# Two-layer graph kernel: new beginning, attention end and end of layer 1's loop

## Chip, cores and metric

One core of a Trainium2 chip runs the whole kernel. The time is device microseconds of one execution; three runs of the kernel before gave 675.48 to 677.48, with a median of 676.37.

## What is computed

```python
# layer 0
deg = clip(adj.sum(axis=1), 1);  dis = deg ** -0.5
diffusion = (dis[:, None] * adj * dis[None, :]) @ x - x
norms = maximum(norm(x), 1e-8)
attn = softmax(beta * (x @ x.T / (norms[:, None] * norms[None, :])) * adj, axis=1)
x = layernorm(x + diffusion + sigmoid(alpha) * (attn @ x - x))
# layer 1
XW = x @ W;  s_col = XW @ a[0, :128];  s_row = XW @ a[0, 128:]
den = exp(leaky_relu(s_row[:, None] + s_col[None, :], 0.01))
num = adj @ den;  att = where(num != 0, den / num, 0)
out = layernorm(x + adj @ (att @ XW))
```

x is 2708 x 128, adj 2708 x 2708 of zeros and ones. The host hands over adj transposed and both padded to 2816 = 22 x 128 rows.

## The kernel before

There are T = 22 tiles of 128 rows (the last has 20) and NC = 6 column pieces of 452 (the last 448). Every engine has its own instruction stream, written out by hand and tied by semaphores; `Waiting.wait_ge` leaves out a wait that an earlier one covers.

**Beginning.** SP loads x (L333), W, a, the row constants, beta and alpha in one queue. POOL issues the 22 loads of adjT, which turn float32 into 8-bit floats in AT (L358): four at once, eighteen after its power. ScalarE squares x (L543), VectorE sums (L786), POOL takes the root by a power (L385), VectorE inverts it and multiplies x by it, four tiles at a time (L800). TensorE transposes the result into two PSUM banks in turn (L1433); ScalarE copies it as float16 (L546), VectorE subtracts this copy for the low half (L797). Then ScalarE makes xh, the bfloat16 copy of x (L547), VectorE and POOL its remainder xl (L806, L389), VectorE the scale of x (`scale_of`, L776 to L782), the sigmoid of alpha and a flag whether beta is large (L810 to L820). Every engine branches on that flag into its `attention` body.

**Layer 0's loop** runs over NU = 132 units, 22 rows jt of six pieces c, through a ring of six buffers. A unit is: three float16 matmuls for the logits on TensorE (L1441), a product with the adjacency on VectorE (L908), Exp on ScalarE (L560), an addition into the row sums ES on POOL (L401; L399 copies in row 0), for four of six pieces the low half of the result on VectorE (L913), and the product with x on TensorE, three bfloat16 matmuls (L1496) or, for the pieces of FULL = (2, 5), one float32 matmul (L1486). In piece 0 of each row 22 one-column matmuls count degrees (L1477), which VectorE adds up (L897). In the last row come the roots of the degrees (`roots`, L855 to L863; Ln and Exp at L563, L565), the scaled x (`scaled`, L869) and its two float16 halves xp (L568, L876).

**Behind the loop** ScalarE and VectorE bring six banks to AOT (L572, L931), POOL splits ES into bfloat16 halves (L416, L418), and TensorE transposes W (L1582), multiplies the first tile's diffusion (`spread(0)`, L1515), transposes AOT (L1596) and sums ES over partitions (`row_sums`, L1571). VectorE needs these sums for all rows of the attention (L987, L991). ScalarE scales x (L591) and later makes `emptied` (L599). The layer norm, the ranking of keys and the windows of layer 1 follow.

**Layer 1's loop** has 66 steps; in each ScalarE takes Ln (L731) and Exp (L709), VectorE the scores (L1322) and the low half (L1329), TensorE sums (L1708) and products (L1768). Behind the branch VectorE multiplies the result (L1378, L1383) into YT, reduces all of it by minimum and maximum (L1387, L1388), combines them (L1390) and calls `scale_of(1, ...)`. TensorE transposes YT meanwhile (L1804), ScalarE and VectorE scale it into two float16 halves (L764, L1395), and 484 matmuls (L1809) give the output, with the layer norm behind each tile.

## Time and profile before

| | |
|---|---|
| median of three runs | 676.37 us |
| the profiled execution | 675.03 us |
| its span, first to last instruction | 673.3 us |
| busy PE, DVE, ACT, POOL | 569.4, 544.2, 352.8, 435.7 us |
| mean granted TensorE clock | 0.944 |

Busy time is given by engine: PE is TensorE, DVE VectorE, ACT ScalarE, POOL GpSimd, SP the queue of plain DMAs. The span leaves out what lies before the first and behind the last instruction, 1.7 us here. A row of the trace names the line of the kernel before.

### The profile page before, as it was taken

What the parts mean: (1) busy time and instruction counts of PE and PEld (TensorE: products, weight loads), DVE (VectorE), ACT (ScalarE), POOL (GpSimd) and SP (SyncE); (2) the same over time, 40 slices, a digit from 0 to 9 for tenths busy, and PEclk for the clock granted to TensorE, in tenths of its full rate; (3) what the DMA queues carried; (4) which work ended last, traced back from release to release, by engine and by line L of the source; (5) the groups of instructions that cost most, each with busy time, mean ns of one, the idle gap of its engine ahead of it and who ended that gap; (6) DMA issues with size and microseconds to landing.
All of it is one profiled execution on the core that took longest, in us unless ns stands there. A gap on an engine that the chain in (4) does not pass through costs nothing.

```text
span 673.3 us, 11277 instructions
## 1 busy us (share of the span) xinstructions
PE 569.4 (85%) x4123; PEld 348.4 (52%) x4123; DVE 544.2 (81%) x965; ACT 352.8 (52%) x568; POOL 435.7 (65%) x448
## 2 busy tenths in 40 slices
PE   0489999999998679999718988898989999949993
PEld 0245555455453368888617644344445444427883
DVE  1679999999999973678888766899898999985442
ACT  2334544444443542579986226787777788811000
POOL 5849999999998933556305043687786788203663
PEclk9999999999999589999757989999999999988997
DMA  9999891000000000000000041323242333000000
GB/s 148 101 108 108 108 380 51 0 1 1 1 1 1 5 1 17 18 24 17 18 1 21 5 125 46 77 82 103 63 110 72 91 95 98 21 5 13 29 28 18
DMA packets 17797, 37.21 MB, mean 55 GB/s; under 512 B 2570, under 2 KB 8222, under 8 KB 17726
## 3 DMA queue, kind: packets, MB, share of 16 engines
q0 software_dynamic: 7392, 24.32, 20.2%
q1 hardware_dynamic: 10334, 11.98, 5.4%
q8 instruction: 39, 0.64, 0.4%
q14 instruction: 32, 0.26, 0.1%
HBM read 48.72 MB, written 10.45 MB: 88 GB/s over the span
## 4 chain that ended last, share of the span: by engine, by line
PE 35%; POOL 25%; DVE 22%; issue 7%; ACT 7%; DMA 2%; DVEq 0%; POOLq 0%; ACTq 0%; SPq 0%
POOL R L401 23%; PE PSALL L1809 8%; PE PSALL L1708 5%; PE PSALL L1515 5%; DVE ring L1329 4%; DVE ring L1322 4%; ACT AW L629 4%; PE PSALL L1637 3%; PE PSALL L1768 3%; PE PSALL L1441 2%; DVE FR L1329 2%; DVE FR L1322 1%; PE PSALL L1716 1%; PE PSALL L1538 1%; DMA X<-in_x 1%
## 5 line engine op out<-in xcount | busy, mean ns | idle before, releaser
L401 POOL TENSOR_TENSOR R<-R,ring 128x452 f32<-128x452 f32 (+1 forms) x126 | 174.9, 1424 | 5.5 <-ACT ring L560 5.5
L560 ACT ACTIVATE ring<-ring,sm 128x452 f32<-128x452 f32 (+1 forms) x132 | 85.0, 669 | 106.0 <-DVE ring L908 105.9
L913 DVE TENSOR_TENSOR AW<-ring 128x452 bf16<-128x452 f32 (+1 forms) x88 | 105.2, 1196 | 0.0
L1441 PE MATMUL PSALL<-XN 128*128 128x452 f16 (+2 forms) x396 | 99.0, 361 | 5.5 <-issue 4.2
L1708 PE MATMUL PSALL<-AW,R 128*128 128x452 fp8e4 (+1 forms) x348 | 78.4, 357 | 16.6 <-DVE R L1261 10.3
L908 DVE TENSOR_TENSOR ring<-PSALL,AT 128x452 f32<-128x452 f32 (+1 forms) x132 | 78.6, 616 | 3.3 <-PE PSALL L1441 2.9
L463 POOL DMA_INDIRECT AW<-ATd,FR x44 | 55.3, 1258 | 31.7 <-DVE FR L1212 17.1
L1768 PE MATMUL PSALL<-ring,XW 128*128 128x452 bf16 (+1 forms) x300 | 67.7, 360 | 0.9 <-DVE ring L1329 0.9
L1441 PEld LDWEIGHTS PSALL<-XN 128*128 128x128 f16 (+1 forms) x396 | 37.6, 98 | 58.1 <-issue 25.4
L1329 DVE TENSOR_TENSOR ring<-ring 128x904 bf16<-128x904 f32 (+1 forms) x50 | 62.6, 1252 | 0.0
L1515 PE MATMUL PSALL<-R,AT 128*128 128x256 f16 x484 | 61.6, 287 | 0.0
L1708 PEld LDWEIGHTS PSALL<-AW,R 128*128 128x128 bf16 x348 | 32.4, 98 | 56.1 <-DVE R L1261 17.2
L1809 PE MATMUL PSALL<-R,AT 128*128 128x256 f16 x484 | 55.1, 279 | 2.0 <-DVE R L1395 2.0
L1496 PE MATMUL PSALL<-ring,AO 128*128 128x452 bf16 (+1 forms) x176 | 50.3, 367 | 4.4 <-DVE AW L913 3.2
L1515 PEld LDWEIGHTS PSALL<-R,AT 128*128 128x128 fp8e4 x484 | 48.8, 103 | 7.8
L1809 PEld LDWEIGHTS PSALL<-R,AT 128*128 128x128 fp8e4 x484 | 48.3, 100 | 8.6 <-DVE R L1395 2.1
L709 ACT ACTIVATE ring<-ring,st 128x904 f32<-128x904 f32 (+1 forms) x50 | 52.3, 1046 | 0.3 <-DVE ring L1322 0.3
L731 ACT ACTIVATE R<-PSALL,sm 128x452 f32<-128x452 f32 x66 | 38.5, 635 | 24.0 <-PE PSALL L1716 20.7
L731 ACT ACTIVATE TL<-PSALL,sm 128x452 f32<-128x452 f32 x66 | 38.5, 635 | 19.7 <-PE PSALL L1716 17.5
L1768 PEld LDWEIGHTS PSALL<-ring,XW 128*128 128x128 bf16 x300 | 28.6, 96 | 31.6 <-DVE ring L1329 2.0
L1322 DVE SCALAR_TENSOR_TENSOR ring<-R,st,TL 128x904 f32<-128x904 f32 (+1 forms) x33 | 38.4, 1162 | 7.2 <-ACT TL L731 6.7
L629 ACT ACTIVATE AW<-R 128x128 bf16<-128x128 bf16 (+21 forms) x30 | 42.7, 1422 | 2.2 <-DVE R L1008 0.4
(262 smaller groups left out, 1035.3 us busy)
## 6 DMA issues: line engine op xcount, KB each, us to landing
AT<-in_adjT POOLq DMA_DIRECT2D x22, 338.5 KB, 32.6
ATd<-AT SPq DMA_DIRECT2D x2, 3723.5 KB, 16.6
XWd<-ring SPq DMA_DIRECT2D x11, 128.0 KB, 1.8
out<-ring SPq DMA_DIRECT2D x21, 64.0 KB, 1.5
AW<-ATd,FR POOLq DMA_INDIRECT x44
X<-XWd,idx POOLq DMA_INDIRECT x22, 2.6
Wt<-in_W SPq DMA_DIRECT2D x1, 64.0 KB, 11.0
X<-in_x SPq DMA_DIRECT2D x1, 0.5 KB, 7.8
```

The source lines that it names most:

```text
L401: i = G.tensor_tensor(ES_, ES_, z, ALU.add)
L560: S.activation(z, z, ACT.Exp, scale=bcol[0:rows, :]).then_inc(s_exp, 1)
L731: S.activation(tL[v % 2][:, q * RW:(q + 1) * RW], PSALL[:, 6 + q, 0:RW], ACT.Ln, bias=tiny).then_inc(s_ln, 1)
L908: V.tensor_tensor(z, PSALL[0:rows, b, 0:w], A_, ALU.mult).then_inc(s_z, 1)
L913: V.tensor_tensor(Fl[q % 6][0:rows, 0:w], ring[0:rows, q % 6, 0:w], upper(q, rows, w), ALU.subtract).then_inc(s_low, 1)
L1322: V.scalar_tensor_tensor(z_of(v), rb[:, c0:c0 + w], negc[:, v // 3:v // 3 + 1], tL[v % 2][:, 0:w], ALU.max, ALU.subtract).then_inc(s_sub, 1)
L1329: V.tensor_tensor(lower, z_of(v), high, ALU.subtract).then_inc(s_alo, 1)
L1441: m = TE.matmul(PSALL[0:rows, b, 0:w], lh[:, jt * P:jt * P + rows], rh[:, c0:c0 + w], start=(k == 0), stop=(k == 2))
L1515: ins = TE.matmul(PSALL[:, it % 4, 0:2 * D], AT[:, jt, it * P:(it + 1) * P], xp[:, jt, :, :].rearrange("p c d -> p (c d)"), start=(jt == 0 ...
L1708: TE.matmul(PSALL[:, b, 0:w], den_h[:, s + 1 + q, :, part], AW[:, jt % 3, q, c0:c0 + w], start=(q == 0 and part == 1), stop=False)
L1768: m = TE.matmul(PSALL[:, c, 0:CH[c][1]], XW2[:, jt % 4, part, :], att[:, part_of], start=(jt == 0 and k == 0), stop=(jt == T - 1 and k == 2))
L1809: return TE.matmul(PSALL[:, out_bank[it], 0:2 * D], AT[:, jt, it * P:(it + 1) * P], xpY[:, jt, :, :].rearrange("p c d -> p (c d)"), start= ...
```

## The change

- x is loaded in two halves, then beta and alpha, then the rest. POOL issues all adjacency loads once both halves of x are there.
- Squares and sums come in four pieces. POOL's power becomes Ln and Exp on ScalarE with a correcting step on VectorE. ScalarE makes two of the six groups of normalised rows; the transposes use four banks; scale, flag and sigmoid are put between the other steps. POOL makes all of xl, the last 18 tiles behind its first six units.
- Logits wait for the low halves that they read, not for all. Degree groups of rows 16 to 21 move to piece 3 of rows 10 to 15.
- Roots move to unit 102. ScalarE makes the scaled x tile by tile in units 105 to 115 and its high halves after that; VectorE makes the low halves in units 121, 123, 127 and 129.
- The last row leaves POOL: its Exp results are split into LH and LL (all six pieces), which TensorE sums with ESh and ESl, 88 matmuls instead of 44. POOL splits ES after 126 units, into other buffers.
- ScalarE takes five banks to AOT, VectorE one. `spread(0)` waits for its bank alone; the transposes of AOT wait for all; the transpose of W comes behind them.
- VectorE's steps from the products of layer 1 to the halves of the result stand inside the branch bodies. ScalarE takes absolute values per pair of pieces, VectorE one maximum each.
- The second semaphore chain s_dve2 becomes s_dve throughout.

```diff
-        ESh, ESl = XN[:, 0:NP // 2].bitcast(BF16)[:, 0:N], XN[:, NP // 2:NP].bitcast(BF16)[:, 0:N]
+        ESh, ESl = EM[:, :].bitcast(BF16)[:, 0:N], AWflat[:, 6 * RW:6 * RW + N]
+        LH, LL = (FR[0:LAST, q * N // 2:(q + 1) * N // 2].bitcast(BF16) for q in range(2))
...
+        QT = ((0, 6), (6, 5), (11, 6), (17, 5))
+        NE = NU - NC
+        DEGREES = {(t, 0): t for t in range(16)}
+        DEGREES.update({(10 + t, 3): 16 + t for t in range(T - 16)})
+        DEG_NO = {u: n for n, u in enumerate(u for u in UNITS if u in DEGREES)}
+        LOWS = [20 * NC + 1, 20 * NC + 3, NE + 1, NE + 3]
+        XD = 17 * NC + 3
...
-            q(X3, x.rearrange("(t p) d -> p t d", p=P)).then_inc(s_x, 16)
+            for h in range(2):
+                q(X3[:, h * 11:(h + 1) * 11, :],
+                  x[h * 11 * P:(h + 1) * 11 * P, :].rearrange("(t p) d -> p t d", p=P)).then_inc(s_x[h], 16)
+            q(braw, beta.broadcast_to([P, 1])).then_inc(s_beta, 16)
+            q(araw, alpha.broadcast_to([P, 1])).then_inc(s_beta, 16)
...
-            for t in range(4):
-                load_AT(t)
...
-            gp.wait_ge(s_sq, 2)
-            G.tensor_tensor(nrm, sq, half.broadcast_to([P, T]), ALU.pow).then_inc(s_norm, 1)
-            for t in range(4, T):
+            for h in range(2):
+                gp.wait_ge(s_x[h], 16)
+            for t in range(T):
                 load_AT(t)
             gp.wait_ge(s_xh, 1)
-            G.tensor_tensor(xl[:, 4:T, :], X3[:, 4:T, :], xh[:, 4:T, :], ALU.subtract).then_inc(s_xlrest, 1)
+            G.tensor_tensor(xl[:, 0:4, :], X3[:, 0:4, :], xh[:, 0:4, :], ALU.subtract).then_inc(s_xlfirst, 1)
+
+            def low_rest(k):
+
+                t0 = 4 + 3 * k
+                G.tensor_tensor(xl[:, t0:t0 + 3, :], X3[:, t0:t0 + 3, :], xh[:, t0:t0 + 3, :], ALU.subtract).then_inc(s_xlrest, 1)
 
             def attention(shifted):
                 if shifted:
...
-                for u, (jt, c) in enumerate(UNITS):
+                for u, (jt, c) in enumerate(UNITS[:NE]):
...
+                    if jt == 0:
+                        low_rest(c)
...
-            gp.wait_ge(s_esum, NU)
-            gp.wait_ge(s_logit, NU)
+            gp.wait_ge(s_esum, NE)
             G.tensor_copy(ESh, ES[:, 0:N]).then_inc(s_es, 1)
             gp.wait_ge(s_es, 1)
             G.tensor_tensor(ESl, ES[:, 0:N], ESh, ALU.subtract).then_inc(s_es, 1)
-            gp.wait_ge(s_aotA, 3)
-            gp.wait_ge(s_aotD, 3)
             G.memset(AOT[:, N:NP], 0.0).then_inc(s_pad, 1)
             for it in range(T):
...
+            av.wait_ge(s_beta, 32)
+            S.activation(eal, araw, ACT.Exp, scale=-1.0).then_inc(s_ealpha, 1)
+            for h, (t0, nt) in enumerate(QT):
+                av.wait_ge(s_x[h // 2], 16)
+                S.activation(xx[:, t0:t0 + nt, :], X3[:, t0:t0 + nt, :], ACT.Square).then_inc(s_early, 1)
+            av.wait_ge(s_sq, 5)
+            S.activation(deg, sq, ACT.Ln).then_inc(s_norm, 1)
+            av.wait_ge(s_norm, 1)
+            S.activation(rn, deg, ACT.Exp, scale=-0.5).then_inc(s_norm, 1)
+
+            def normal_rows(g):
+
+                t0, nb = GRP[g]
+                av.wait_ge(s_sq, 6)
+                for t in range(t0, t0 + nb):
+                    i = S.activation(AO3[:, t, :], X3[:, t, :], ACT.Copy, scale=rn[:, t:t + 1])
+                i.then_inc(s_early, 1)
+
+            def rows_high(g):
+
+                t0, nb = GRP[g]
                 av.wait_ge(s_xnT, g + 1)
-                S.activation(xnh[:, t0 * P:(t0 + nb) * P], PSALL[:, g % 2, 0:nb * P], ACT.Copy).then_inc(s_xnh, 1)
+                S.activation(xnh[:, t0 * P:(t0 + nb) * P], PSALL[:, g % 4, 0:nb * P], ACT.Copy).then_inc(s_xnh, 1)
+
+            normal_rows(1)
...
+            normal_rows(1)
+            rows_high(0)
+            normal_rows(4)
+            for g in range(1, 6):
+                rows_high(g)
             S.activation(xh, X3, ACT.Copy).then_inc(s_xh, 1)
...
+            def scaled_rows(t0, nt):
+
+                av.wait_ge(s_dis, 4)
+                for t in range(t0, t0 + nt):
+                    S.activation(xd3[:, t, :], X3[:, t, :], ACT.Copy, scale=dup[:, t:t + 1]).then_inc(s_xd, 1)
+
+            def scaled_high(k):
+
+                t0, nt = SL[k]
+                av.wait_ge(s_xd, t0 + nt)
+                S.activation(xp[:, t0:t0 + nt, 0, :], xd3[:, t0:t0 + nt, :], ACT.Copy).then_inc(s_xphi, 1)
 
...
+                    if not shifted and 0 <= u - XD < T // 2:
+                        scaled_rows(2 * (u - XD), 2)
+                    if not shifted and 0 <= u - XD - T // 2 < len(SL):
+                        scaled_high(u - XD - T // 2)
+                    if jt == T - 1:
+                        av.wait_ge(s_exp, u + 1)
+                        S.activation(LH[:, CH[c][0]:CH[c][0] + w], upper(u, rows, w), ACT.Copy).then_inc(s_lh, 1)
...
+                for c in range(NC - 1):
                     c0, w = CH[c]
+                    av.wait_ge(s_gather, NE + c + 1)
                     S.activation(AOT[:, c0:c0 + w], PSALL[:, c, 0:w], ACT.Copy).then_inc(s_aotA, 1)
...
+            av.wait_ge(s_rsum, 1)
...
+            for p in range(3):
+                c0, w = wide_of(p)
+                av.wait_ge(s_YTd, 2 * p + 2)
+                S.activation(YA[:, c0:c0 + w], YT[:, c0:c0 + w], ACT.Abs).then_inc(s_yhi, 1)
...
+            V.tensor_scalar(sq, sq, COS_EPS * COS_EPS, None, ALU.max).then_inc(s_sq, 1)
+            dv.wait_ge(s_beta, 32)
+            V.tensor_scalar(bcol, braw, 1.0 / (XS * XS), None, ALU.mult).then_inc(s_bcol, 1)
+            k = own.step(V.tensor_tensor(beta2, braw[0:1, :], braw[0:1, :], ALU.mult))
             dv.wait_ge(s_dve, k)
-            k = own.step(V.reciprocal(rn, nrm))
+            k = own.step(V.tensor_scalar(beta2, beta2, BETA_PLAIN ** 2, None, ALU.is_gt))
             dv.wait_ge(s_dve, k)
-
-            def split_low(g):
+            V.tensor_copy(flag[:, :], beta2).then_inc(s_flag, 1)
+            dv.wait_ge(s_norm, 2)
+            k = own.step(V.tensor_tensor(dis, rn, rn, ALU.mult))
+            dv.wait_ge(s_dve, k)
+            k = own.step(V.tensor_tensor(dis, dis, sq, ALU.mult))
+            dv.wait_ge(s_dve, k)
+            k = own.step(V.tensor_scalar(dis, dis, -0.5, 1.5, ALU.mult, ALU.add))
+            dv.wait_ge(s_dve, k)
+            V.scalar_tensor_tensor(rn, dis, XS, rn, ALU.mult, ALU.mult).then_inc(s_sq, 1)
+            dv.wait_ge(s_sq, 6)
+
...
+            normal_rows(0)
+            k = own.step(V.scalar_tensor_tensor(nrm, sq, 1.0 / (XS * XS), rn, ALU.mult, ALU.mult))
+            normal_rows(2)
+            dv.wait_ge(s_dve, k)
             V.tensor_reduce(pm, nrm, AX.X, ALU.max).then_inc(s_pm, 1)
-            scale_of(0, (PSALL[0:1, 5, 0:P], PSALL[:, 5, 0:1]), XS, up_x, down_x)
+            rows_low(0)
+            normal_rows(3)
+            dv.wait_ge(s_scale, 1)
+            k = own.step(V.tensor_reduce(top, PSALL[0:1, 5, 0:P], AX.X, ALU.max))
+            rows_low(1)
+            dv.wait_ge(s_dve, k)
+            V.tensor_scalar(top, top, 1e-30, None, ALU.max).then_inc(s_top, 1)
+            normal_rows(5)
+            rows_low(2)
+            rows_low(3)
+            dv.wait_ge(s_scale, 2)
+            k = own.step(V.tensor_scalar(down_x, PSALL[:, 5, 0:1], XS * 2.0 ** -14, None, ALU.mult))
+            rows_low(4)
+            dv.wait_ge(s_dve, k)
+            V.reciprocal(up_x, down_x).then_inc(s_up, 1)
+            rows_low(5)
             dv.wait_ge(s_ealpha, 1)
             k = own.step(V.tensor_scalar(eal, eal, 1.0, None, ALU.add))
             dv.wait_ge(s_dve, k)
...
+                    if u == 17 * NC:
+                        roots()
+                    if not shifted and u in LOWS:
+                        scaled_low(LOWS.index(u))
...
+            def products_out():
+
+                dv.wait_ge(s_sub, NV)
+                dv.wait_ge(s_erb, 1)
+                for p in range(3):
+                    c0, w = wide_of(p)
+                    dv.wait_ge(s_y, NV - 3 + p + 1)
+                    if w == 2 * RW:
+                        V.tensor_tensor(YT[:, c0:c0 + w].rearrange("p (q w) -> p q w", q=2), PSALL[:, 2 * p:2 * p + 2, 0:RW],
+                                        erb[:, c0:c0 + w].rearrange("p (q w) -> p q w", q=2), ALU.mult).then_inc(s_YTd, 2)
+                    else:
+                        for c in (2 * p, 2 * p + 1):
+                            c0, w = CH[c]
+                            V.tensor_tensor(YT[:, c0:c0 + w], PSALL[:, c, 0:w], erb[:, c0:c0 + w], ALU.mult).then_inc(s_YTd, 1)
+                    if p == 0:
+                        V.memset(orow, 1.0)
+                for p in range(3):
+                    c0, w = wide_of(p)
+                    dv.wait_ge(s_yhi, p + 1)
+                    k = own.step(V.tensor_reduce(ln[:, p:p + 1], YA[:, c0:c0 + w], AX.X, ALU.max))
+                dv.wait_ge(own.sem, k)
+                V.tensor_reduce(pm, ln[:, 0:3], AX.X, ALU.max).then_inc(s_pm, 1)
+
+            def transposed_out():
+
+                scale_of(1, (PSALL[0:1, 6, 0:P], PSALL[:, 6, 0:1]), 1.0, up_y, down_y)
+                dv.wait_ge(s_up, 2)
+                for g, (t0, nb) in enumerate(GRP):
+                    dv.wait_ge(s_yhi, 3 + g + 1)
+                    V.scalar_tensor_tensor(xpY[:, t0:t0 + nb, 1, :], PSALL[:, g, 0:nb * P].rearrange("p (b d) -> p b d", b=nb), up_y,
+                                           xpY[:, t0:t0 + nb, 0, :], ALU.mult, ALU.subtract).then_inc(s_ylo, 1)
 
             table(2)
             where["any"] = eng.value_load(win[0:1, 2 * T:2 * T + 1], min_val=0, max_val=1)
...
-            own.step(V.tensor_reduce(up_y, YT, AX.X, ALU.min))
-            k = own.step(V.tensor_reduce(down_y, YT, AX.X, ALU.max))
-            dv.wait_ge(s_dve2, k)
-            V.scalar_tensor_tensor(pm, up_y, -1.0, down_y, ALU.mult, ALU.max).then_inc(s_pm, 1)
...
+            turn(0)
+            turn(1)
+            pe.wait_ge(s_pm, 1)
+            TE.transpose(PSALL[0:1, 5, 0:P], pm, ident[:, :]).then_inc(s_scale, 1)
+            turn(2)
+            turn(3)
+            pe.wait_ge(s_top, 1)
+            TE.matmul(PSALL[:, 5, 0:1], orow, top, start=True, stop=True).then_inc(s_scale, 1)
+            turn(4)
+            turn(5)
 
...
-                pe.wait_ge(s_xnl, 6)
+                pe.wait_ge(s_xnl, max((c0 + w - 1) // (4 * P), jt // 4) + 1)
...
+                if it < 4:
+                    pe.wait_ge(s_aotA, it + 1)
...
+                pe.wait_ge(s_aotA, NC - 1)
+                TE.transpose(PSALL[:, 4, 0:P], Wt[:, :], ident[:, :]).then_inc(s_wT, 1)
                 pe.wait_ge(s_es, 2)
+                pe.wait_ge(s_lh, NC)
+                pe.wait_ge(s_low, low_no(NU - 1))
+                pe.wait_ge(s_aotD, 1)
                 for t in range(T):
                     rows = rows_of(t)
-                    for k, part in enumerate((ESh, ESl)):
-                        m = TE.matmul(PSALL[0:rows, 5, t:t + 1], part[:, t * P:t * P + rows], ones[:, :],
-                                      start=(k == 0), stop=(k == 1))
+                    for k, (part, high) in enumerate(((ESh, P), (ESl, P), (LH, LAST), (LL, LAST))):
+                        m = TE.matmul(PSALL[0:rows, 5, t:t + 1], part[0:high, t * P:t * P + rows], ones[0:high, :],
+                                      start=(k == 0), stop=(k == 3))
                 m.then_inc(s_rsum, 1)
```

## Rows read from the trace of the kernel before

**Rows 1.** Page, chain that ended last, shares by line

```profile
POOL R L401 23%; PE PSALL L1809 8%; PE PSALL L1708 5%; PE PSALL L1515 5%; DVE ring L1329 4%; DVE ring L1322 4%; ACT AW L629 4%; PE PSALL L1637 3%; PE PSALL L1768 3%; PE PSALL L1441 2%; DVE FR L1329 2%; DVE FR L1322 1%; PE PSALL L1716 1%; PE PSALL L1538 1%; DMA X<-in_x 1%
```

**Rows 2.** Chain of waits in order, beginning: start us, us, what

```profile
0.86 7.82 DMA X<-in_x
...
13.35 3.91 POOL st L385
...
34.85 1.04 issue
```

**Rows 3.** Timeline, beginning: start, us, engine, line, out<-in, count [idle before]

```profile
26.66 1.02 DVE L797 TENSOR_TENSOR XN<-PSALL,XN 128x512 f16<-128x512 f32 x2 [0.90 <-ACT XN L546]
...
29.44 5.04 POOL L389 TENSOR_TENSOR AO<-X,AO 128x2304 bf16<-128x2304 f32 x1 [2.61 <-ACT AO L547]
...
37.95 0.61 DVE L908 TENSOR_TENSOR ring<-PSALL,AT 128x452 f32<-128x452 f32 x1
```

**Rows 4.** DMA issues (last column us to landing); start of the ATd stores

```profile
sm<-in_alpha SPq DMA_DIRECT2D x1, 0.5 KB, 19.7
...
L339 SPq DMA_DIRECT2D ATd<-AT x2: 389/914/1439, 82.2 to 82.6; - x2
```

**Rows 5.** Timeline inside layer 0's loop, VectorE one row apart; POOL's in an early row

```profile
101.86 0.61 DVE L908 TENSOR_TENSOR ring<-PSALL,AT 128x452 f32<-128x452 f32 x1
...
110.03 0.61 DVE L908 TENSOR_TENSOR ring<-PSALL,AT 128x452 f32<-128x452 f32 x1
...
46.56 1.15 POOL L401 TENSOR_TENSOR R<-R,ring 128x452 f32<-128x452 f32 x1 [1.27 <-ACT ring L560]
```

**Rows 6.** Chain of waits in the loop's first rows, degree groups

```profile
44.44 0.53 PE PSALL L1477 x22
...
52.38 0.54 PE PSALL L1477 x22
```

**Rows 7.** Timeline, the end of layer 0's attention

```profile
195.34 16.87 POOL L401 TENSOR_TENSOR R<-R,ring 128x452 f32<-128x452 f32 x12
...
212.84 1.01 DVE L855 TENSOR_TENSOR st<-st 128x22 f32<-128x22 f32 x1
...
215.42 0.24 DVE L863 TENSOR_SCALAR st<-st,sm 128x22 f32<-128x22 f32 x1
...
222.94 3.61 DVE L876 TENSOR_TENSOR R<-R 128x768 f16<-128x768 f32 x3
...
223.57 1.70 PE L1486 MATMUL PSALL<-ring,X 20*128 20x448 f32 x2
...
225.80 3.06 POOL L416 CAST XN<-R 128x2708 bf16<-128x2708 f32 x1
...
228.49 4.75 PE L1515 MATMUL PSALL<-R,AT 128*128 128x256 f16 x22
...
234.64 1.33 PE L1571 MATMUL PSALL<-ones,XN 128*128 128x1 bf16 x44 [0.52 <-POOL XN L418]
...
236.65 6.54 ACT L599 ACTIVATE EM<-ident,FR 128x128 bf16<-128x128 f32 x22
```

**Rows 8.** Windows: busy us of PE, PEld, DVE, ACT, POOL, granted clock, DMA, GB/s

```profile
180.00:200.00 20.00, 19.78 (x149) 9.98 (x147) 20.00 (x31) 9.54 (x15) 20.00 (x16) 1.00 0.00 1
...
226.00:236.00 10.00, 7.22 (x76) 5.61 (x76) 8.78 (x8) 4.09 (x7) 8.63 (x3) 0.65 0.02 5
```

**Rows 9.** Page's group L709; timeline at the end of layer 1

```profile
L709 ACT ACTIVATE ring<-ring,st 128x904 f32<-128x904 f32 (+1 forms) x50 | 52.3, 1046 | 0.3 <-DVE ring L1322 0.3
...
591.33 2.58 PE L1768 MATMUL PSALL<-ring,XW 128*128 128x452 bf16 x12 [0.95 <-DVE ring L1329]
...
594.49 2.11 DVE L1378 TENSOR_TENSOR R<-PSALL,R 128x904 f32<-128x904 f32 x2 [2.00 <-PE PSALL L1768]
...
597.72 3.06 DVE L1387 TENSOR_REDUCE sm<-R 128x1 f32<-128x2816 f32 x1
...
603.81 0.16 DVE L1390 SCALAR_TENSOR_TENSOR sm<-sm 128x1 f32<-128x1 f32 x1
```

236 lines of the change are left out of this document (96 added, 140 removed).

## Prediction

> **What bounds the kernel now.** I read the chain of waits by line first, then the timeline where the change touches it. The chain puts the largest share, 23%, on POOL's additions of layer 0 (L401) [rows 1]. So the reader should see three places: the stretch before that loop, its last row with what follows it, and the end of layer 1.
>
> The beginning is a single file. X arrives at 8.68 us, POOL's power starts behind the squares and their sums at 13.35 and takes 3.91 us, and the last transposed low half (L797) ends at 27.68 [rows 2, 3]. Only then come xh, the scale and a chain of tiny VectorE steps, and from 34.85 on 1.04 us for the branch into the loop body [rows 2]. The first masked logit piece (L908) starts at 37.95 [rows 3].
>
> In the loop a row of six units takes 8.17 us (101.86 to 110.03) [rows 5]. Early, while POOL has slack, TensorE alone sets 7.94 us a row: its two degree groups start that far apart in an unbroken PE chain [rows 6]. One POOL addition with little beside it took 1.15 us [rows 5], so six take 6.90; the four low halves (L913) of a row raise it to 8.17, as I read it, by (8.17-6.90)/4 = 0.32 us each. TensorE, VectorE and POOL are thus within a few per cent of one another, and no one of them relieved alone gives much.
>
> POOL's twelve-unit block ends at 212.21, then five slow units follow, since VectorE's small dependent steps (L855, 1.01 us) and its scalings sit between them; the conversion of the row sums starts at 225.80 and ends where the 44 summing matmuls begin, 234.64 [rows 7]. These end at 235.97. At the end of layer 1 the last product ends at 593.91, the multiplications start at 594.49, two full reductions run from 597.72, and the maximum is ready at 603.97 [rows 9].
>
> **Beginning.** X comes in two halves and POOL issues no adjacency load before both are there. Alpha and beta are queued behind X alone; before, alpha was issued last and took 19.7 us [rows 4]. ScalarE now waits for both ahead of its squares, so I let it start at 9.0, 0.3 later than before. Squares and sums in four pieces: the first sum starts after a smaller square, all end near 13.2, as before. POOL's 3.91 us becomes a clip, Ln and Exp of 22 columns, a hand-over each way and four small steps, seven things of 0.2 to 0.24 (L863 [rows 7]) and 0.2 for hand-overs: 1.8 us. The four beta steps lie in ScalarE's shadow. rn is ready at 15.0 instead of 17.8. From there VectorE has the six low halves (0.68 for 512 columns, by L797's 1.02 for 768 [rows 3]; 3.8 in all), four groups of normalised rows of the same size (2.5) and 1.1 us of scale steps, 7.4 us, and I add 0.8 us for waits on ScalarE, which has two groups of rows (8 x 0.3 by L599's 6.54/22 [rows 7]) and six copies: last low half at 23.2. Then the two sigmoid steps and the branch of 1.04: the first L908 at 25.2, **12.8 us earlier**. xh runs after ScalarE's copies, beside it, to about 24.2; POOL waited 2.61 us on it before [rows 3].
>
> Adjacency: the 22 loads were all in when the first store to ATd was issued, at 82.2 [rows 4]; issued from 3.5 us on, they took near 3.5 us each. Issued from 9 us on they end near 89; row t is wanted at 25+8.2t and comes at 15+3.5t, so this costs nothing. The two stores to ATd move with them and are first read after 380 us.
>
> POOL pays: xl (5.04 us for 18 tiles [rows 3]) and the other four tiles, 1.1 us, were hidden before its first unit. Now the 1.1 us stand ahead of the loop and 0.84 us behind each of its first six copies. Its row 0 ends at about 35.4, where the old pace from 25.2 would give 33.8; of the 1.6 us, early idle time takes up 0.6. **Cost 1.0.**
>
> **Loop.** The degree group is 0.53 us [rows 6]. Six move from rows 16 to 21 into rows 10 to 15, where TensorE then needs 7.94+0.53 = 8.47 us against 8.17: 6 x 0.30 = 1.8, and 0.2 of VectorE's additions. **Cost 2.0**; rows 16 to 20 give nothing back, as POOL and VectorE keep 8.17. The scaled rows go to ScalarE, 22 x 0.3 = 6.6 us, and four high copies, in units where it was half idle. They cost nothing unless two units come close together; bounds 0 to 2 us, taken 0. VectorE gets the roots (five steps, 212.84 to 215.66 [rows 7]) in row 17 and four low halves of xp (1.2 each [rows 7]) in the last two rows. How much of that POOL feels has no row: at best its ring cushion takes all (0), at worst all of it passes through, 2.85+4.8 = 7.7 us. The nearest is the low half's 0.32 us where L908, of the same width, takes 0.61 [rows 5], half: **cost 4.0**.
>
> A low half thus lengthened the row by a third of a microsecond. The Trainium skill, "SBUF — State Buffer", section "Who interferes with whom", has VectorE and POOL take the shared pair of ports by a lock for a whole instruction when both read SBUF. By it all 4.8 us of the low halves of xp would pass, and the total would be about 2 us more than mine. The trace agrees that they lengthen each other, not with the full length.
>
> **End of layer 0.** POOL stops after 126 units. Unit 125 ended about 210.5 (212.21 less the block's last unit, 126; the block's mean is 1.41). It now ends at 210.5-12.8+1.0+2.0+4.0 = 204.7. The conversion is unchanged, 8.8 us: 213.6. TensorE's last row has three matmuls in each unit; z of the last unit can follow unit 125's addition, then Exp, low half, product: last product near 208.5. Before, 3.2 us passed from the last product (225.27) to spread(0) at 228.49 [rows 7], with VectorE's copies and a short transpose in them; I take 2.9 for leaving the branch. spread(0) then runs 211.4 to 216.1 at the price of [rows 7], 4.75 us; the granted clock there was 0.65 [rows 8], part of the time at the 1.2 GHz level. Two groups of transposes bring 217.2, the transpose of W and 88 sums instead of 44 (2 x 1.33) bring 219 to 220; at the 2.4 GHz level spread(0) is 2.4 us shorter and they end near 217.6. I take 219.0: **17.0 us earlier** than 235.97. ScalarE's copy of W now follows spread(0), and its scaling of X (2816 columns, 3.2 us by L709's rate [rows 9]) ends by 218.5, in time for VectorE's first subtraction, but with under 1 us to spare. The wait for the row sums put before the 22 copies of emptied costs nothing: they already started after them.
>
> The middle, 236 to 591, is untouched and moves as a block.
>
> **End of layer 1.** The code stays in the branch body, so the 2.00 us that VectorE was idle before the multiplications [rows 9] go. It can multiply piece 0 at 592.5; the third is bound by the last product (593.91) and ends at 595.9. ScalarE's absolute values (L709's 1.05 us for 904 columns [rows 9]) end at 597.4. The maxima of the three pieces, 1.0 us each by a third of a full reduction (3.0), run from 595.9 to 598.9, the last small one to 599.1, against 603.97: **4.9 us**. Minimum and combination are gone. TensorE's 22 transposes end near 599.2 and the maximum's transpose follows: **4.7 us** taken. The output matmuls start that much earlier and run as long as before.
>
> **Sum.** 17.0+4.7 = 21.7 us. The profiled execution took 675.03 us (span 673.3), so 653.3 for it; the median is 676.37, 1.3 above, so 654.7.
>
> **Rivals.**
> (a) The loop takes the beginning's gain back in part. For it: VectorE and POOL have no idle time from 180 to 200 us [rows 8], and ScalarE's added work delays Exp when two logit pieces come together. Against it: the ring holds six units. With all 7.7 us of [rows 7], 2 for ScalarE and 2 for a late alpha (if an adjacency load gets ahead of it in the rings, 3.5): 661. Chance 0.2.
> (b) More gain: the cushion takes roots and low halves (4.0 less) and TensorE holds 2.4 GHz into spread(0) (1.4 less): 649. Chance 0.15.
> (c) The end gives nothing, because ScalarE needs as long as VectorE to get out of the body and absolute values and maxima follow in file: 3 us of 4.7 lost, 657.7. Chance 0.06, inside the range.
> (d) Slower than before: TensorE's granted clock. From 180 to 200 us it was 1.00, the 2.4 GHz level; where the engine had idled it was 0.65 [rows 8]. VectorE's inserted steps starve TensorE in rows 17 to 21, and if the clock then stays at 1.2 GHz, a row costs up to 15.9 instead of 8.17 us. Three such rows eat 23 us and decide the sign; four give 654.7+31 = 686. Against it: within the loop TensorE also had its waits and the clock stayed. The Trainium skill, "TensorE: Matmul & The Clock Gate", Part 1, ties the level to how busy the engine has lately been, in agreement with [rows 8]. Chance 0.04.
> (e) The change does not do what it says: a new wait, such as spread(0) for W or the four low halves, holds the row sums at their old distance from the loop. Then the beginning's 12.8 less 7, and 4.7: 665.9. Chance 0.02.
> The forecast itself, 651 to 658, has 0.53.
>
> **Range and chances.** From (b) to (a): 648 to 662. A measurement of this kernel tells about 0.3%, 2 us. Faster by more: 0.96; same 0.01; slower 0.03; these two share (d)'s chance, by three rows or more.
>
> **What would show it.** First L908 at 25 (over 28: alpha late or the transposes dearer); POOL unit 125 ending 179.5 us after it (over 183: rival a; under 176: b); rows 10 to 15 at 8.5 us; the summing matmuls ending at 219; from the last product to the maximum 5.2 us instead of 10.1. Wrong would be: granted clock under 1.00 between 30 and 200 us, a wait for AT in the loop, or a middle stretch that changes its length by over 1 us.

## The result, and the profile after

The changed kernel takes 667.74 us (four runs, 666.92 to 668.91) against 675.92 in the four runs of the kernel before on the same chip: ratio 0.9887, 95% interval 0.9864 to 0.9911. It is faster, by 8.2 us where 21.7 was forecast, and lies outside the range. The profiled execution took 667.40 us, its span 665.6, the mean granted clock is 0.944 as before.

I follow a few marks through both traces, all in us from the start of the span. The last two columns say how long the way from the mark above took.

| mark | before | after | way, before | way, after |
|---|---|---|---|---|
| first masked logit piece starts | 37.95 | 24.53 | | |
| POOL's unit 125 ends | 210.72 | 202.79 | 172.8 | 178.3 |
| last product of the attention ends | 225.27 | 218.52 | 14.6 | 15.7 |
| VectorE takes the row sums | 236.01 | 232.77 | 10.7 | 14.2 |
| last product of layer 1 ends | 593.91 | 590.89 | 357.9 | 358.1 |
| first output matmul | 607.55 | 600.30 | 13.6 | 9.4 |
| end of the span | 673.3 | 665.6 | 65.8 | 65.3 |

The prediction took unit 125 of the kernel before at 210.5; POOL's timeline has the next unit start where it ended:

```profile
210.69 1.52 POOL L401 TENSOR_TENSOR R<-R,ring 20x452 f32<-20x452 f32 x1
```

13.4 us are won at the beginning. The loop gives 5.5 back, the two ways behind it 1.2 and 3.5, the middle 0.2; the end of layer 1 brings 4.2, what follows it 0.5. The page's chain by line shows the same shift: POOL's additions fall from 23% [rows 1] to 10%, and VectorE's masked pieces (L998) and low halves (L1003) and TensorE's products (L1600) take part of their place.

```profile
POOL R L427 10%; PE PSALL L1919 8%; PE PSALL L1621 6%; PE PSALL L1818 5%; DVE ring L1410 4%; DVE ring L1403 4%; PE PSALL L1544 3%; PE PSALL L1747 3%; ACT AW L696 3%; PE PSALL L1878 3%; PE PSALL L1600 3%; DVE ring L998 3%; DVE AW L1003 2%; DVE FR L1410 2%; DVE FR L1403 1%
```

**Beginning**, timeline (start, us, engine, line, operation, out<-in, count). It answers to [rows 2, 3].

```profile
8.59 0.20 ACT L567 ACTIVATE sm<-sm 128x1 f32<-128x1 f32 x1 [6.51 <-DMA sm<-in_alpha]
...
9.56 3.27 DVE L857 TENSOR_REDUCE st<-AO 128x6 f32<-128x768 f32 x4 [9.56 <-ACT AO L570]
...
14.22 0.18 DVE L874 SCALAR_TENSOR_TENSOR st<-st 128x22 f32<-128x22 f32 x1
...
22.44 0.41 DVE L888 TENSOR_TENSOR XN<-PSALL,XN 128x256 f16<-128x256 f32 x1
...
24.53 1.15 DVE L998 TENSOR_TENSOR ring<-PSALL,AT 128x452 f32<-128x452 f32 x2
```

The sums end at 12.83 (9.56+3.27), rn is there at 14.40 and the last low half at 22.85. This is the file of the prediction, 0.4 to 0.7 us ahead of it.

It holds a wait that could go. ScalarE takes the exponential of alpha (L567) ahead of the squares, and the chain of waits leads through alpha's load, not through x:

```profile
4.70 3.87 DMA sm<-in_alpha
...
8.59 0.20 ACT sm L567
8.79 0.74 ACT AO L570
```

The two halves of x were issued at 0.80 and 1.32 and took 5.1 and 6.9 us, so they lay there at 5.9 and 8.2, while the first square started at 8.70. Squares put ahead of the exponential could have begun on the first half about 2.8 us earlier; what that would bring was not run.

**Attention end**, timeline. It answers to [rows 7].

```profile
202.85 3.05 POOL L443 CAST EM<-R 128x2708 bf16<-128x2708 f32 x1
...
204.07 2.32 DVE L1003 TENSOR_TENSOR FR<-ring 20x452 bf16<-20x452 f32 x1
...
205.99 5.63 POOL L445 TENSOR_TENSOR AW<-R,EM 128x2708 bf16<-128x2708 f32 x1
206.31 0.61 DVE L998 TENSOR_TENSOR ring<-PSALL,AT 20x452 f32<-20x452 f32 x1
...
206.85 5.25 DVE L1003 TENSOR_TENSOR FR<-ring 20x452 bf16<-20x452 f32 x1
...
212.16 0.93 PE L1600 MATMUL PSALL<-ring,AO 20*128 20x452 bf16 x2 [4.29 <-DVE FR L1003]
...
217.95 0.57 PE L1600 MATMUL PSALL<-FR,AO 20*128 20x448 bf16 x1
218.56 0.62 DVE L1014 COPY R<-PSALL 128x448 f32<-128x448 f32 x1 [2.64 <-PE PSALL L1600]
...
221.03 4.75 PE L1621 MATMUL PSALL<-R,AT 128*128 128x256 f16 x22 [2.51 <-issue]
...
226.60 0.17 PE L1682 MATMUL PSALL<-ones,EM 128*128 128x1 bf16 x1
...
226.62 0.16 PE L1682 MATMUL PSALL<-ones,AW 128*128 128x1 bf16 x1
...
226.72 0.20 PE L1682 MATMUL PSALL<-ones,FR 20*128 20x1 bf16 x2
...
226.85 0.18 PE L1682 MATMUL PSALL<-ones,EM 128*128 128x1 bf16 x1
```

Two things are to be seen. Two low halves of the last row (L1003), which take 0.61 us with POOL idle, take 2.32 and 5.25 and end 0.4 to 0.5 us after POOL's two splitting instructions; the piece of L998 between them, which reads one operand from PSUM, keeps 0.61. TensorE sits idle 4.29 us behind the longer one. And the 88 summing matmuls (L1682) come four in 0.26 to 0.29 us, so the 22 tiles last from 226.60 to 232.66, where the next matmul starts: 6.1 us where [rows 7] had 1.33 for 44.

Windows: busy PE, PEld, DVE, ACT, POOL, granted clock, DMA, GB/s.

```profile
120.00:140.00 20.00, 20.00 (x189) 11.14 (x188) 18.50 (x35) 9.28 (x14) 20.00 (x16) 1.00 0.01 1
...
180.00:200.00 20.00, 17.28 (x75) 6.70 (x73) 20.00 (x25) 13.64 (x27) 19.70 (x14) 1.00 0.00 1
213.00:221.00 8.00, 5.15 (x14) 1.47 (x13) 3.55 (x7) 4.64 (x9) 0.00 (x0) 0.50 0.03 6
221.00:233.00 12.00, 11.97 (x121) 9.94 (x122) 0.57 (x5) 3.36 (x5) 0.00 (x0) 0.64 0.01 2
```

In the loop the granted clock is 1.00, the 2.4 GHz level, also where VectorE's added steps leave TensorE 2.7 of 20 us idle. Behind the long idle time it is at the 1.2 GHz level (0.50), and the products of the last units take 0.57 where they took 0.35.

**End of layer 1**, timeline. It answers to [rows 9].

```profile
588.33 2.56 PE L1878 MATMUL PSALL<-ring,XW 128*128 128x452 bf16 x12 [0.95 <-DVE ring L1410]
589.37 1.08 DVE L1450 TENSOR_TENSOR R<-PSALL,R 128x904 f32<-128x904 f32 x1
...
590.49 3.11 ACT L831 ACTIVATE R<-R 128x904 f32<-128x904 f32 x3 [2.26 <-DVE R L1450]
...
592.53 3.07 DVE L1461 TENSOR_REDUCE ln<-R 128x1 f32<-128x904 f32 x3
593.13 3.60 PEld L1914 LDWEIGHTS PSALL<-ident,R 128*128 128x128 f32 x22 [2.69 <-DVE R L1455]
593.14 4.00 PE L1914 MATMUL PSALL<-ident,R 128*128 128x128 f32 x22 [2.24 <-DVE R L1455]
595.64 0.16 DVE L1463 TENSOR_REDUCE sm<-ln 128x1 f32<-128x3 f32 x1
596.72 0.13 PEld L1510 LDWEIGHTS PSALL<-ident,sm 128*1 128x1 f32 x1
...
600.30 2.10 PE L1919 MATMUL PSALL<-R,AT 128*128 128x256 f16 x12 [2.02 <-DVE R L1471]
```

The first multiplication starts before the last product ends, and the maximum is ready at 595.80, 4.9 us behind the last product instead of 10.1. But the 22 transposes took 4.00 us instead of 2.63, and the maximum's own transpose stands behind them. The granted clock was 0.63 from 593.1 to 597.2, and 1.00 in the same stretch of the kernel before.

### The profile page after: what moved, and what is told of

It reads as the page before. It is cut to its first block, busy times and chain, and to the rows that moved or that the text cites. A ratio compares the mean times of both kernels' runs of the same rounds, so it can differ in the third digit from the quotient of the medians.

```text
span 665.6 us, 11419 instructions
## 1 busy us (share of the span) xinstructions
PE 573.8 (86%) x4169; PEld 353.2 (53%) x4169; DVE 527.7 (79%) x965; ACT 369.8 (56%) x613; POOL 424.3 (64%) x447
## 4 chain that ended last, share of the span: by engine, by line
PE 44%; DVE 26%; POOL 12%; issue 9%; ACT 6%; DMA 1%; SPq 1%; DVEq 0%; POOLq 0%; ACTq 0%
POOL R L427 10%; PE PSALL L1919 8%; PE PSALL L1621 6%; PE PSALL L1818 5%; DVE ring L1410 4%; DVE ring L1403 4%; PE PSALL L1544 3%; PE PSALL L1747 3%; ACT AW L696 3%; PE PSALL L1878 3%; PE PSALL L1600 3%; DVE ring L998 3%; DVE AW L1003 2%; DVE FR L1410 2%; DVE FR L1403 1%
## 5 line engine op out<-in xcount | busy, mean ns | idle before, releaser
L427 POOL TENSOR_TENSOR R<-R,ring 128x452 f32<-128x452 f32 x120 | 164.2, 1406 | 2.4 <-ACT ring L618 2.4
L618 ACT ACTIVATE ring<-ring,sm 128x452 f32<-128x452 f32 (+1 forms) x132 | 86.5, 669 | 92.2 <-DVE ring L998 91.8
L1003 DVE TENSOR_TENSOR AW<-ring 128x452 bf16<-128x452 f32 x84 | 94.4, 1124 | 0.0
L998 DVE TENSOR_TENSOR ring<-PSALL,AT 128x452 f32<-128x452 f32 (+1 forms) x132 | 79.5, 616 | 7.0 <-PE PSALL L1544 6.3
L1600 PE MATMUL PSALL<-ring,AO 128*128 128x452 bf16 (+1 forms) x180 | 52.7, 374 | 7.8 <-DVE FR L1003 5.1
L455 POOL TENSOR_SCALAR ln<-ln 128x1 f32<-128x1 f32 (+1 forms) x22 | 13.2, 599 | 59.6 <-DVE ln L1060 59.6
```

Source lines behind the costliest of these rows:

```text
L427: i = G.tensor_tensor(ES_, ES_, z, ALU.add)
L618: S.activation(z, z, ACT.Exp, scale=bcol[0:rows, :]).then_inc(s_exp, 1)
L998: V.tensor_tensor(z, PSALL[0:rows, b, 0:w], A_, ALU.mult).then_inc(s_z, 1)
L1003: V.tensor_tensor(low_of(q)[0:rows, :], ring[0:rows, q % 6, 0:w], upper(q, rows, w), ALU.subtract).then_inc(s_low, 1)
L1600: m = TE.matmul(PSALL[:, c, 0:w], half_[0:rows, jt, :], att, start=(jt == 0 and k == 0), stop=(jt == T - 1 and k == 2))
```

## The experiments

Each kernel is the changed one with the edit shown. All ratios are to the kernel before, whose median on the same chip stood at 676.0 or 676.1, and at 674.0 beside four kernels (old beginning, two sums, split in pieces, pieces and body), which are best compared by their ratios. The changed kernel again, as a level, gave 667.34, ratio 0.9877 [0.9858, 0.9897]. Its second profile (span 667.2) differs from the first in two places that matter below: the middle took 360.3 us instead of 358.1, and the way from the last product of layer 1 to the first output matmul 8.2 us instead of 9.4.

> The changed kernel itself beside the others: 667 to 668.5, and 0.987 to 0.990 of the kernel before. Nothing tells theories apart here; it is the level for the other three.

### The split of ES kept away from the last row

```diff
             gp.wait_ge(s_esum, NE)
+            gp.wait_ge(s_low, low_no(NU - 1))
             G.tensor_copy(ESh, ES[:, 0:N]).then_inc(s_es, 1)
```

> The changed kernel with one wait more: POOL begins its split of the row sums (3.05 and 5.63 us) only when VectorE's last low half of the attention is done. Theory P (POOL's two long instructions hold the ports that VectorE needs for the small low halves of the last row; in the changed kernel one of them took 5.25 us instead of 0.61 and another 2.32): all low halves of the last row take 0.6 to 1.1 us, the last product of the attention ends near 210 instead of 218.5, the row sums end near 225 instead of 232.7, and the whole is 5 to 8 us faster than the changed kernel (660 to 663) although POOL starts later. Theory T (the last row is slow because TensorE's clock is low there, and POOL's split is not what VectorE waits for): the low halves keep their length, the split ends 8 us later, and the kernel is as fast as the changed one or slower by up to 4 us. Rival S (the split's own end is what counts): 3 to 6 us slower.

661.42 us, 0.9799 [0.9759, 0.9839]: 5.9 less than the changed kernel. Timeline:

```profile
206.97 0.61 DVE L1004 TENSOR_TENSOR FR<-ring 20x452 bf16<-20x452 f32 x1
...
209.91 2.44 POOL L444 CAST EM<-R 128x2708 bf16<-128x2708 f32 x1 [6.97 <-DVE FR L1004]
...
211.65 0.62 DVE L1015 COPY R<-PSALL 128x448 f32<-128x448 f32 x1 [1.87 <-PE PSALL L1601]
...
214.56 4.85 PE L1622 MATMUL PSALL<-R,AT 128*128 128x256 f16 x22 [2.94 <-issue]
214.69 3.21 DVE L1033 TENSOR_SCALAR FR<-st 128x22 f32<-128x22 f32 x1 [2.41 <-issue]
...
226.63 0.18 DVE L1038 COPY st<-PSALL 128x21 f32<-128x21 f32 x1 [8.69 <-PE PSALL L1683]
```

All low halves of the last row take about 0.6 us again, the last product ends at 211.62, 6.9 us earlier, and the row sums come at 226.63, 6.1 earlier, although POOL's split now starts 7 us later. Its second instruction still overlaps something: a VectorE step of 22 columns (L1033), 0.18 us in the changed kernel, takes 3.21; nobody waits for it.

Cutting the split into six pieces of 452 columns instead leaves it where it is and shortens the time that VectorE is held.

```diff
-            G.tensor_copy(ESh, ES[:, 0:N]).then_inc(s_es, 1)
-            gp.wait_ge(s_es, 1)
-            G.tensor_tensor(ESl, ES[:, 0:N], ESh, ALU.subtract).then_inc(s_es, 1)
+            for c, (c0, w) in enumerate(CH):
+                G.tensor_copy(ESh[:, c0:c0 + w], ES[:, c0:c0 + w]).then_inc(s_es, 1)
+                gp.wait_ge(s_es, 2 * c + 1)
+                G.tensor_tensor(ESl[:, c0:c0 + w], ES[:, c0:c0 + w], ESh[:, c0:c0 + w], ALU.subtract).then_inc(s_es, 1)
```

> The changed kernel with POOL's split in six pieces of 452 columns, twelve instructions of 0.5 to 1.1 us instead of two of 3.05 and 5.63. It starts where it did. Theory P (one long POOL instruction keeps VectorE out for all its length): no low half of the last row waits over 1.1 us, the last product ends at 211 to 213 instead of 218.5, the split ends near 214, and the kernel is 5 to 7 us faster than the changed one, as with the late split. Rival: it is the amount of POOL's work that slows VectorE, in pieces or not, and the last product stays near 217.

663.69 us, 0.9821 [0.9777, 0.9865]. The last row's low halves take 0.61 to 1.46 us, the last product ends at 213.76 and the row sums come at 228.95. By the ratios this is 3.8 of the 5.3 us that the late split gives, less than the 5 to 7 expected, but the intervals of the two overlap; by the traces the last product is 4.8 us earlier than in the changed kernel, with the late split 6.9.

### The 88 summing matmuls

Without the split, ES summed whole in float32:

```diff
-                    for k, (part, high) in enumerate(((ESh, P), (ESl, P), (LH, LAST), (LL, LAST))):
+                    for k, (part, high, unit) in enumerate(((ES, P, onec), (LH, LAST, ones), (LL, LAST, ones))):
```

> The changed kernel without POOL's split: TensorE sums ES itself in float32 (22 matmuls of one column against a column of ones) beside the 44 small ones of the last row. Theory P: no long POOL instruction stands beside the last row, the last product ends near 209, the row sums near 222, 8 to 11 us faster than the changed kernel (657 to 660). Theory T: the last product stays near 218 and only what waits for the split changes, at most 1 us. For the sums themselves: 22 float32 matmuls are two passes each, so 88 passes as before; at the clock level of the changed kernel (0.64 in that window) 6 us, at the full level about 3.

668.20 us, 0.99 [0.9868, 0.9932], runs from 663.75 to 669.46, where 657 to 660 was expected. The last product ends at 210.48, which confirms the split's part, but the sums now take 11.3 us (219.3 to 230.7) and the row sums come at 230.85. I had thought of a float32 column as two cheap ones.

Only ESh and ESl summed; the 20 nodes of the last row are left out of the softmax sums:

```diff
-                    for k, (part, high) in enumerate(((ESh, P), (ESl, P), (LH, LAST), (LL, LAST))):
+                    for k, (part, high) in enumerate(((ESh, P), (ESl, P))):
```

> The changed kernel without the sums over LH and LL: the last row's 20 nodes are left out of the softmax sums, 44 matmuls in the place of 88, all waits as they were. The 88 took 6.0 us in the changed kernel at a granted clock of 0.64, 68 ns each; the 44 of the kernel before took 1.33 us, 30 ns each. Theory: the last row's sums cost 3.0 us at the low clock, and this kernel is 3 us faster than the changed one (664.7), its 44 sums still at 60 to 68 ns. Rival: the length is set by something else (the small matmuls themselves pull the clock down), and the 44 run at 30 ns: then 4.7 us faster.

662.92 us, 0.9813 [0.977, 0.9856]. The last product ends at 218.52 as in the changed kernel, the row sums come at 228.06, 4.7 us earlier. The 44 sums follow each other every 0.03 us, 1.3 in all (226.71 to 228.02).

So half of the matmuls takes a fifth of the time. What differs is the height: LH and LL have 20 rows. The changed kernel's own trace says more: the second 128-row sum of a tile starts 0.04 us after the first (226.85 to 226.89), the 20-row sum 0.10 after that (226.62 to 226.72), its like 0.04 behind it, and the next tile's first 128-row sum 0.09 later. So a 20-row sum is not dear in itself; the two changes of height in each tile are. The next kernel keeps all 88 and makes them equally high, with zeros below (on top of the late split; `gp`'s zeros are written while it waits for x):

```diff
+            G.memset(FR[:, 0:N], 0.0).then_inc(s_iota, 1)
...
-                    for k, (part, high) in enumerate(((ESh, P), (ESl, P), (LH, LAST), (LL, LAST))):
+                    for k, (part, high) in enumerate(((ESh, P), (ESl, P), (LHp, P), (LLp, P))):
```

> The kernel with the late split, and LH and LL filled up with zeros to 128 partitions (a memset by POOL while it waits for x), so that all 88 sums contract over 128 partitions; the result is the same. In the changed kernel 88 sums, half of them over 20 partitions, took 6.0 us (68 ns each); the 44 sums over 128 partitions took 1.33 us before and about as little where the 20-row sums were left out, at much the same granted clock. Theory M (going back and forth between 20 and 128 rows costs time at each change): 88 full sums take 2.7 to 3.0 us, the row sums end 3.0 us earlier, 658.5. Rival C (it is the clock level): they take 5 to 6 us again and the time stays at 661 to 662.

658.32 us, 0.9744 [0.9721, 0.9766]: 3.1 less than the late split alone. Its timeline, TensorE and VectorE:

```profile
220.03 0.17 PE L1688 MATMUL PSALL<-ones,EM 128*128 128x1 bf16 x1
220.06 0.16 PE L1688 MATMUL PSALL<-ones,AW 128*128 128x1 bf16 x1
...
222.38 0.59 PE L1692 MATMUL PSALL<-ac,ring 128*128 128x2 f32 x2
222.49 0.18 DVE L1042 COPY st<-PSALL 128x21 f32<-128x21 f32 x1 [4.95 <-PE PSALL L1688]
```

88 sums from 220.03 to 222.38, where the next matmul starts, 2.35 us, and the row sums at 222.49, 4.1 us earlier than with the late split alone. The same number of matmuls, 27 ns each instead of 69. The two windows differ in the granted clock too (0.97 here, 0.72 with the late split alone), but that is not the cause: with the split in pieces and the body (below) the sums of unequal height ran at 0.95 and still took 5.9 us.

```profile
219.47:225.35 5.88, 5.88 (x91) 4.94 (x88) 0.00 (x0) 3.36 (x5) 0.00 (x0) 0.95 0.01 3
```

### The branch

`spread(0)`, its transposes and the sums inside TensorE's branch body, on top of the split in pieces:

```diff
+            def opening():
+
+                for t in range(T):
+                    pe.wait_ge(s_AT[t], 16)
+                pe.wait_ge(s_w, W_IN)
+                spread(0)
+                turns(0)
+                row_sums()
...
                         m.then_inc(s_gather, 1)
+                opening()
```

> As the kernel with pieces, and TensorE does spread(0), the two groups of transposes and the row sums inside its branch body, before it leaves it. In the changed kernel 2.5 us lie between the last product and spread(0), and what follows runs at the low clock: 4.75 us where spread takes 2.4 at the upper level, 6.0 us for the 88 sums. Theory C (idle time of TensorE around the branch's end lets the clock fall): spread(0) begins within 0.3 us of the last product, the clock stays higher, the sums end 3 to 8 us earlier than with pieces alone: 653 to 658. Rival: the clock is already low in the last row, because TensorE waits there, and only the 2.5 us go: 658 to 660. Second rival: the 2.5 us come back behind the row sums, where TensorE leaves the branch then: 0 to 1 us faster than with pieces alone.

663.47 us, 0.9812 [0.9764, 0.986], the same as the pieces alone. `spread(0)` starts at 214.28, without a gap, and the row sums come at 225.38, 3.6 us earlier. But TensorE leaves the body behind them, and the next product of a diffusion is late by it:

```profile
228.85 3.36 PE L1571 MATMUL PSALL<-R,AT 128*128 128x256 f16 x17 [2.99 <-issue]
```

`spread(1)` started 0.34 us behind the row sums with the pieces alone, and 3.47 here. The gap is moved, not removed.

The same on top of the equally high sums, with the later transposes ahead of their `spread` (shown against the kernel just described):

```diff
                 if it:
-                    spread(it)
                     turns(it)
+                    spread(it)
```

> As the kernel with full rows, with spread(0), its transposes and the sums inside TensorE's branch body, and each later pair of transposes ahead of its spread. In the kernel with pieces and body the row sums ended 3.6 us earlier and spread(1) began 3.5 us behind them instead of 0.3; what it won it gave back, since the next transposes stood behind spread(1). Theory: the way out of the branch now lies beside VectorE's 2.8 us for the first rows; the sums end at 220.5 to 221.5 (the split ends at 217.7), and the stretch behind them stays at 358 to 361: 2 to 5 us faster than with full rows, 654 to 656. Rival: the stretch behind the sums is longer by the way out again, 0 to 1 us faster.

656.10 us, 0.9699 [0.9679, 0.9719]: 2.2 less than with the equally high sums alone. The row sums come at 220.90.

### The end of layer 1

The end of the kernel before (behind the branch, two full reductions) in the changed kernel:

```diff
                 attention_low(NV - 1)
-                products_out()
-                transposed_out()
...
+            own.step(V.tensor_reduce(up_y, YT, AX.X, ALU.min))
+            k = own.step(V.tensor_reduce(down_y, YT, AX.X, ALU.max))
```

> The changed kernel with layer 1's end as before: products behind the branch, minimum and maximum over the whole result, no absolute values. In the traces the way from the last product to the first output matmul is 13.6 us before (593.91 to 607.55) and 9.4 after (590.89 to 600.30). Theory: this part is worth 4.2 us and nothing else, so 671.9, 4.2 above the changed kernel, and about 3.8 us faster than the kernel before. Rival: the beginning and the attention's end (3.1 us in the traces) are what the clocks vary by, and this kernel is level with the changed one or with the one before.

672.68 us, 0.9962 [0.9936, 0.9988], twelve runs from 669.98 to 675.92, in the median about 5 us more than the changed kernel. From the last product to the first output matmul pass 13.5 us, against 9.4 and 8.2 in the two profiles of the changed kernel, so the new end is worth 4.1 to 5.3 us by the traces.

The new end, but behind the branch:

```diff
                 attention_low(NV - 1)
-                products_out()
-                transposed_out()
...
             dv.only(met)
+            products_out()
+            transposed_out()
```

> The changed kernel's new steps at the end of layer 1 (absolute values on ScalarE, one maximum per piece), but VectorE's part of them stands behind the branch, as it did before. Theory: leaving the branch costs VectorE the 2.00 us idle of the trace before, of which the wait for the last product hides up to 1.4; the maximum is 1 to 1.5 us later, and TensorE's slow transposes (4.0 us, 593.1 to 597.1), behind which the maximum's transpose waited 1.1 us, hide part: 0.3 to 1.5 us over the changed kernel. Rival: the place is all of the gain, 4 us over it.

669.01 us, 0.9918 [0.9887, 0.9949], about 1.5 more, which by the intervals is hardly clear of noise. VectorE's idle time is back, and the maximum is ready at 597.58, 6.9 us behind the last product instead of 4.9:

```profile
591.16 1.10 DVE L1448 TENSOR_TENSOR R<-PSALL,R 128x904 f32<-128x904 f32 x1 [1.90 <-PE PSALL L1878]
```

The first output matmul comes 10.2 us behind the last product, 0.8 later than in the changed kernel's first profile, whose transposes were as slow (4.0 us, 4.3 here). So the single maximum per piece carries most of the gain, and the place inside the body a fifth (traces) to a third (times).

Last, on top of the kernel with the body, the maximum's transpose between the groups of YT's transposes:

```diff
                 m.then_inc(s_YTT, 1)
-            scale_of(1, 6)
+                if g == 2:
+                    pe.wait_ge(s_pm, 2)
+                    TE.transpose(PSALL[0:1, 6, 0:P], pm, ident[:, :]).then_inc(s_scale, 1)
+                if g == 3:
+                    pe.wait_ge(s_top, 2)
+                    TE.matmul(PSALL[:, 6, 0:1], orow, top, start=True, stop=True).then_inc(s_scale, 1)
```

> As the last one, with the transpose of layer 1's maximum between TensorE's third and fourth group of transposes and the spreading of the maximum behind the fourth. In the changed kernel the maximum was ready at 595.80 and its transpose waited until 596.93 behind 22 transposes at the low clock. Theory: the first output matmul comes 1.0 us earlier relative to the last product (9.4 to 8.4 us), 653 to 655. Rival: the two groups left over delay ScalarE's copies by as much, no change.

654.67 us, 0.9691 [0.9674, 0.9709], which is not clear of noise against the 0.9699 of the kernel with the body. The maximum's transpose starts 0.06 us after it is ready, and from the last product (577.85) to the first output matmul pass 8.15 us:

```profile
582.57 0.15 DVE L1468 TENSOR_REDUCE sm<-ln 128x1 f32<-128x3 f32 x1
582.78 0.08 PEld L1934 LDWEIGHTS PSALL<-ident,sm 128*1 128x1 f32 x1 [1.30 <-DVE sm L1468]
...
586.00 22.09 PEld L1940 LDWEIGHTS PSALL<-R,AT 128*128 128x128 fp8e4 x190 [1.46 <-DVE R L1476]
```

This doesn't show that the edit works. The granted clock in the stretch of the transposes was 1.00, and where it was 1.00 the kernels without the edit took as little: the changed kernel's second profile 8.19 us, the late split 8.15, the equally high sums 8.17, each with transposes of 2.6 us, and there the maximum's transpose started within 0.1 us too. Only where the transposes took 4.0 us (granted clock 0.63 or 0.64) did the maximum's transpose wait for them, and the way took 9.1 to 9.4. Whether the edit saves that 1 us in such an execution, no trace shows.

This version beats both kernels: 13 us under the changed one, 21 under the one before.

### The old beginning

The changed kernel with the beginning of before on all engines: x in one load, POOL's power, SP's queue with alpha last, xl of the last 18 tiles in one.

```diff
-            for h in range(2):
-                gp.wait_ge(s_x[h], 16)
-            for t in range(T):
+            gp.wait_ge(s_sq, 2)
+            G.tensor_tensor(nrm, sq, half.broadcast_to([P, T]), ALU.pow).then_inc(s_norm, 1)
+            for t in range(4, T):
                 load_AT(t)
```

> The changed kernel with the beginning of the kernel before: x in one piece, alpha and beta last, POOL's power, groups of normalised rows on VectorE alone, two banks, all of xl ahead of the loop. By the traces the first masked logit piece is 13.4 us earlier in the changed kernel (37.95 to 24.53), and the loop from there to POOL's unit 125 is 5.7 us longer (172.6 to 178.3). Theory: what of the 5.7 us is POOL's xl in row 0 (I said 1.0) belongs to the beginning, the rest to the steps put into the last rows; so this kernel reaches unit 125 at 215 and is 12 to 13 us slower than the changed kernel, 680, slower than the kernel before by 4. Rival: the loop takes back what the beginning gives, since three engines are equally full; then the kernel is slower by 7 us or less, at most 675.

681.35 us, 1.0092 [1.0062, 1.0123]: slower than the kernel before. The first masked piece starts at 37.70, unit 125 ends at 215.84, a way of 178.1 us with all of xl ahead of the loop, 5.4 more than before. POOL's timeline shows how the two kernels come to nearly the same sum. Times are from the first masked piece to the end of POOL's addition (in row 0 its copy):

| POOL's last unit of | before | changed | old beginning |
|---|---|---|---|
| row 0 | 7.34 | 10.43 | 7.55 |
| row 9 | 82.68 | 85.26 | 83.05 |
| row 15 | 131.79 | 133.99 | 133.30 |
| row 17 | 148.16 | 152.19 | 151.56 |
| row 20 | 172.77 | 178.26 | 178.14 |

In the changed kernel xl makes POOL 3.1 us later in row 0, and 2.6 are still there after row 9. With this backlog the degree groups of rows 10 to 15 cost POOL nothing: it even regains 0.4. Without it they cost 1.1 us. So xl is not free, and its price and the degrees' hide in each other; that the end comes out equal within 0.1 us doesn't price xl alone. Across the kernels that share the changed kernel's loop this way took 178.3 to 179.1 us.

The new beginning alone is worth about 14.5 us (by the ratios, 1.0092 less 0.9877 of 676; with their intervals about 12 to 17), and the rest of the change as it stands, without it, loses. The lock is there too:

```profile
218.43 5.89 POOL L437 TENSOR_TENSOR AW<-R,EM 128x2708 bf16<-128x2708 f32 x1
...
219.62 5.18 DVE L950 TENSOR_TENSOR FR<-ring 20x452 bf16<-20x452 f32 x1
```

## Why the prediction was wrong

**Beginning: right.** 12.8 us taken, 13.4 measured. The small steps between sums and rn took 1.57 us (12.83 to 14.40) of the 1.8 allowed.

**Loop: near in its sum, partly by luck.** From the first piece to unit 125 I had 179.5, measured 178.3; 7.0 us were forecast as its price and 5.5 came, by the table under the old beginning. I had 1.0 for xl and 2.0 for the degree groups, as if they added up: xl took 3.1 in row 0, and after row 15 both together stood at 2.2. TensorE did have its longer rows there: from row 10's first masked piece to row 16's 51.2 us instead of 49.1, 2.0 more as forecast, with TensorE and POOL both 20.00 of 20 us busy. I had 4.0 for the roots and four low halves of xp: the roots cost 1.8 in row 17, where POOL stood idle, and the two low halves of row 20 cost 1.4.

```profile
169.84 29.86 POOL L427 TENSOR_TENSOR R<-R,ring 128x452 f32<-128x452 f32 x21 [2.05 <-ACT ring L618]
```

The other two low halves lie behind unit 125, in the last row, where I had charged nothing for them. Unit 125 ended 1.9 us earlier than forecast.

**End of layer 0: the step that failed.** I wrote of the split that "the conversion is unchanged, 8.8 us", and of the last row "last product near 208.5". That is 3.8 us behind unit 125; it measured 15.7, and the row sums came at 232.8 instead of 219.0. The parts:

- 6.9 us are VectorE waiting for POOL. The change takes POOL out of the last row, so the split that had run behind VectorE's last steps now runs beside them, and I had given it no neighbour. I had weighed the Trainium skill's rule ("SBUF — State Buffer", "Who interferes with whom") for the low halves of xp only: VectorE and POOL take a shared pair of ports by a lock for a whole instruction, when VectorE reads both inputs from SBUF and POOL reads SBUF too. Here the trace agrees with the rule: 5.25 us for a step of 0.61, ended 0.5 us after the end of the 5.63 us split, and 0.61 for the step with one operand in PSUM. The late split shows the cause: without the overlap the last product is 6.9 earlier.
- 5.0 us remain with the late split (202.94 to 211.62, 8.7 us against 3.8). I had let the last unit follow unit 125's addition at once. But the z pieces of units 126 to 131 start 200.38, 201.87, 203.68, 204.75, 206.43 and 207.56, some 1.4 us apart, with the low halves of xp (1.35 and 0.67) between them and VectorE busy without a break from 200 to 209, and the last products run at the lower clock, the window from 209 to 212 granted 0.60. How the 5.0 us divide between the two, no run shows.
- 3.4 us are the sums: priced 2 x 1.33 = 2.7, measured 6.1. Padding the 20 rows to 128 takes it back to 2.35.
- 0.3 us is the rest of that way; leaving the branch (2.5 us idle for 2.9 forecast) and `spread(0)` (4.75 for 4.75) came as priced, and the 219.0 that I took was 0.9 under the sum of its own steps (208.5+2.9+4.75+1.1+2.66 = 219.9).

Together 6.9+5.0+3.4+0.3 = 15.6, less the 1.9 that unit 125 was early: 13.7 of the 14.1 us by which the profiled execution (667.40) missed its forecast of 653.3.

**Middle: right in the first profile**, 358.1 for 357.9, but not a block. The changed kernel's second profile has 360.3, over the 1 us that I had named as a sign of being wrong, and most experiments have 359.6 to 360.6. One source is TensorE's clock. Both profiles of the changed kernel reach 391.41 at the same time and after the same wait for a gather; the first goes on at a granted clock of 1.00 (390 to 395), the second at 0.53:

```profile
391.41 1.69 PE L1818 MATMUL PSALL<-AW,R 128*128 128x452 fp8e4 x8 [2.98 <-DMA AW<-ATd,FR]
...
391.41 3.17 PE L1818 MATMUL PSALL<-AW,R 128*128 128x452 fp8e4 x8 [2.99 <-DMA AW<-ATd,FR]
```

The first scores of layer 1's loop (L1403) then start at 394.64 and 396.31. So a gain ahead of the middle is not passed on in full in each execution: the late split's 6.1 us at the row sums are 3.9 at the last product of layer 1. Why the clock fell in one execution and not in the other is open.

**End of layer 1: right in size, with another remainder.** 4.7 taken, 4.2 measured; the maximum came 4.9 us behind the last product (5.2 forecast). The rest went to TensorE's transposes, 4.00 us for the 2.6 I had assumed, which kept the maximum's transpose 1.1 us. In the second profile, at a granted clock of 1.00, they took 2.63 and kept nothing; there the way is 5.4 us shorter than before.

**The rivals.** None gave the reason. (a) was refuted: the loop cost less than my own forecast. (Its terms, 3.7, 2 and 2 on 654.7, give 662.4 and not 661.) (b) had the ring's cushion take the roots and low halves, and they cost 1.8 and 1.4 us. (d) did not happen inside the loop; the granted clock stayed 1.00. (c) did not hold, since ScalarE's absolute values ran beside the multiplications. (e), "a new wait" between loop and row sums, at 665.9 and with a chance of 0.02, was nearest in place and number, but named `spread(0)` for W and xp, and not VectorE behind POOL. That its chance was so small is the error of judgement: the new order of that stretch had no rows of before, and I had ends only for the loop.

## What to carry to other kernels

When a step is taken off an engine, look at what that engine does next and beside whom it now runs: POOL, freed of a row, started a 5.6 us instruction into VectorE's critical steps, and one wait that let it start later made the kernel 5.9 us faster. A long instruction with SBUF operands on POOL belongs beside VectorE work that nobody waits for, or is cut into pieces. Chains of one-column matmuls should have the same height throughout; here zeros were cheaper than a change of height. And the costs of two additions to one pipeline are not to be added up: a delay on one engine can hide a delay on another.

## What the runs showed of the hardware that I had not expected

- The lock hits the smallest steps as hard: a VectorE step of 22 columns took 3.21 us instead of 0.18 beside POOL's 5.31 us subtraction (the late split), and 3.87 in the kernel with the body and equally high sums.
- One-column bf16 matmuls: 27 to 30 ns each when all have 128 rows (88 in 2.35 us, 44 in 1.33), 69 ns when pairs of 128 and of 20 rows alternate. Start to start, at a granted clock of 1.00, two sums of the same height are 0.04 us apart in that chain, of 128 rows or of 20; from 128 to 20 rows pass 0.10 us, and back 0.09. At 0.50 a tile takes 0.29 us instead of 0.26, so the clock is the smaller part. Which part of TensorE this is was not taken apart.
- Float32 sums of one column are not two cheap ones: the trace has 44 float32 passes for the 22 sums, and at a granted clock of 1.00 the second starts 0.13 us after the first, where bf16 sums of equal height follow every 0.025. With ES whole the sums took 11.3 us, changes of height and a clock that fell to 0.56 on the way (from 223.5 on) included.
- Leaving a branch body cost TensorE 1.3 us (the old beginning) to 3.9 (whole sums) of idle time that waited for nothing the profile shows (2.51 in the changed kernel) and VectorE 1.9 to 2.8. Moved behind the sums it was paid there.
- The same kernel, at the same instruction and after the same wait of 3 us, went on at a granted clock of 1.00 in one execution and 0.53 in another: 1.69 or 3.17 us for eight matmuls.
